# Which engine multiplies the queries by the cosine: GpSimd or VectorE

## The reference

```python
def apply_rope(x):                       # per head of 32 channels
    x1, x2 = (x[..., ::2], x[..., 1::2])
    out = jnp.stack([x1 * cos - x2 * sin, x1 * sin + x2 * cos], axis=-1)
    return out.reshape(x.shape)
q = heads(x @ Wq.T + bq)
k = heads(x @ Wk.T + bk)
v = heads(x @ Wv.T + bv)
g = jax.nn.sigmoid(heads(x @ Wg.T + bg))
q = jax.nn.elu(apply_rope(q)) + 1.0
k = jax.nn.elu(apply_rope(k)) + 1.0
...
S = S + jnp.einsum('bhtd,bhte->bhde', ki, vi)      # a running state, chunks of 64 tokens
num = jnp.einsum('bhtd,bhde->bhte', qi, S)
den = jnp.einsum('bhtd,bhd->bht', qi, Z)[..., None] + 1e-06
out = g * num / den                                # then out @ Wo.T + bo
```

## Time and profile before

| | |
|---|---|
| time, median of 3 runs | 1132.95 us (1131.48 to 1133.48) |
| the profiled execution, its own time | 1128.95 us |
| its span | 1127.1 us |
| busy: PE, PEld, DVE, ACT, POOL | 91%, 72%, 64%, 36%, 26% |
| POOL L443, 64 instructions of 128x256 | 893 ns mean |
| POOL L447, 16 instructions of 128x512 | 21.6 us in all, 1349 ns mean |
| DVE L762, 16 instructions of 128x512 | 12.4 us in all, 775 ns mean |
| DVE L767, 32 instructions of 128x512 | 40.1 us in all, 1254 ns mean |

### The profile page before, as it was taken

One profiled execution on the slowest core, in us unless ns is written; L12 is line 12 of the kernel. 1 busy time (PEld: TensorE's weight loads), 2 busy tenths in 40 slices (PEclk: granted clock), 3 DMA queues, 4 the chain that ended last, 5 costly groups with the idle time before them and its releaser, 6 DMA issues.

```text
span 1127.1 us, 13755 instructions
## 1 busy us (share of the span) xinstructions
PE 1030.8 (91%) x4920; PEld 809.6 (72%) x4920; DVE 717.8 (64%) x1150; ACT 402.7 (36%) x623; POOL 295.3 (26%) x245
## 2 busy tenths in 40 slices
PE   3799999989999827999999899999999999999997
PEld 2577777767777625777768687777777877888885
DVE  4565786785576646957657867764976774554542
ACT  3234333323342233344443253434253434322231
POOL 2247674543224400201222200142110132200021
PEclk9899999999999968999999999999999999999999
DMA  7116664130021025243463152446143327134421
GB/s 261 62 61 232 214 232 146 61 104 10 10 92 31 1 78 225 99 161 111 163 219 123 39 210 103 170 158 233 39 158 134 133 79 276 57 140 154 172 66 56
DMA packets 47862, 142.98 MB, mean 127 GB/s; under 512 B 3497, under 2 KB 14633, under 8 KB 42161
## 3 DMA queue, kind: packets, MB, share of 16 engines
q1 hardware_dynamic: 28720, 118.71, 28.8%
q10 hardware_dynamic: 19072, 23.35, 6.4%
HBM read 114.66 MB, written 27.39 MB: 126 GB/s over the span
## 4 chain that ended last, share of the span: by engine, by line
PE 44%; DVE 13%; issue 3%; ACT 2%; POOL 1%; DMA 1%; DVEq 0%; ACTq 0%
PE f_h L106 7%; PE f_h L107 7%; PE f_h L108 7%; PE f_h L2172 4%; PE f_y L106 3%; PE f_y L107 3%; PE f_y L108 3%; DVE f_q_mem L1933 2%; DVE f_work L1913 1%; PE f_y L2362 1%; DVE f_work L1905 1%; PE f_z_sum L106 1%; PE f_z_sum L108 1%; PE f_z_sum L107 1%; PE f_z_second L107 1%
## 5 line engine op out<-in xcount | busy, mean ns | idle before, releaser
L106 PE MATMUL f_h<-f_xT_hi,f_up 128*128 128x512 f32 x352 | 140.5, 399 | 1.6 <-issue 0.9
L107 PE MATMUL f_h<-f_xT_hi,f_up 128*128 128x512 f32 x352 | 138.4, 393 | 0.0
L108 PE MATMUL f_h<-f_xT_lo,f_up 128*128 128x512 f32 x352 | 137.7, 391 | 0.0
L106 PE MATMUL ring<-w_hi,xT_hi 128*128 128x512 f32 x256 | 110.4, 431 | 24.4 <-POOL xT_lo L429 21.8
L1505 POOL TENSOR_TENSOR f_down_lo<-f_down_raw,f_down_hi 128x512 fp32r<-128x512 f32 x44 | 61.1, 1390 | 227.5 <-ACT f_down_hi L1555 227.5
L1710 ACT ACTIVATE f_work<-f_h 128x512 f32<-128x512 f32 x88 | 52.4, 596 | 171.4 <-PE f_h L2172 114.8
L1905 DVE TENSOR_TENSOR f_work<-f_work,f_weightT 128x512 f32<-128x512 f32 x88 | 65.1, 739 | 73.7 <-ACT f_work L1710 69.9
L1516 POOL TENSOR_TENSOR weights<-weights,f_rows 128x512 f32<-128x512 f32 (+1 forms) x24 | 31.9, 1360 | 299.9 <-ACT f_rows L1637 183.6
L1913 DVE TENSOR_TENSOR f_work<-f_h,f_work 128x512 f32<-128x512 f32 x88 | 60.8, 691 | 70.8 <-PE f_h L108 65.3
L107 PE MATMUL ring<-w_hi,xT_lo 128*128 128x512 f32 x256 | 103.7, 405 | 0.0
L108 PE MATMUL ring<-w_lo,xT_hi 128*128 128x512 f32 x256 | 103.5, 404 | 0.0
(11 more groups left out here) (306 smaller groups left out, 2244.0 us busy)
## 6 DMA issues: line engine op xcount, KB each, us to landing
f_up<-up_scratch SPq DMA_DIRECT2D x44, 1408.0 KB, 6.2
f_down_raw<-in_down_stream ACTq DMA_DIRECT2D x44, 256.0 KB, 3.6
f_x<-x_scratch SPq DMA_DIRECT2D x7, 1024.0 KB, 8.8
scaled_w<-in_up_stream SPq DMA_DIRECT2D x6, 704.0 KB, 5.4
up_scratch<-q_mem SPq DMA_DIRECT2D x6, 704.0 KB, 3.6
up_scratch<-scaled_w SPq DMA_DIRECT2D x6, 704.0 KB, 3.1
x_tok<-in_x SPq DMA_DIRECT2D x4, 1024.0 KB, 5.6
out<-f_x SPq DMA_DIRECT2D x8, 512.0 KB, 3.1
```

Of the source, the lines that this page charges most:

```text
L106: pe.matmul(out, lhs_hi, rhs_hi, start=start, stop=False)
L107: pe.matmul(out, lhs_lo, rhs_hi, start=False, stop=False)
L108: return pe.matmul(out, lhs_hi, rhs_lo, start=False, stop=stop)
```

## The change

The product of the queries with the cosine goes from GpSimd's `rotate` to VectorE's `rotated_sum`, which now does the same for queries and keys: it waits for the copy out of PSUM, makes the product, and then waits for the products with the sine (before, the keys' product stood behind that wait).

```diff
@@ rotate (GpSimd)
                     pool.tensor_tensor(b4[:, :, :, two], q4[:, :, :, 1 - two],
                                        sin[:, :, two].unsqueeze(1).to_broadcast([P, H, DK // 2]),
                                        ALU.mult).then_inc(rot_b_ready, 1)
-                if i == 0:
-                    pool.tensor_tensor(rot_a[:, 0:D].rearrange("p (h i) -> p h i", i=DK),
-                                       qk[:, 0:D].rearrange("p (h i) -> p h i", i=DK),
-                                       ropes[:, 0, t, :].unsqueeze(1).to_broadcast([P, H, DK]), ALU.mult)\
-                        .then_inc(rot_a_ready, 1)
@@ rotated_sum (VectorE)
                 half = bass.ts(i, D)
                 n = 2 * g + i + 1
+                k, _, done = own(g, (PQ, PK)[i])
+                dve.wait_ge(drained[k], PRIMED + done)
+                dve.tensor_tensor(rot_a[:, half].rearrange("p (h i) -> p h i", i=DK),
+                                  qk[:, half].rearrange("p (h i) -> p h i", i=DK),
+                                  ropes[:, 0, in_batch(g), :].unsqueeze(1).to_broadcast([P, H, DK]), ALU.mult)\
+                    .then_inc(rot_a_ready, 1)
+                dve.wait_ge(rot_a_ready, PRIMED + n)
                 dve.wait_ge(rot_b_ready, PRIMED + 2 * n)
-                if i:
-                    k, _, done = own(g, PK)
-                    dve.wait_ge(drained[k], PRIMED + done)
-                    dve.tensor_tensor(rot_a[:, half].rearrange("p (h i) -> p h i", i=DK),
-                                      qk[:, half].rearrange("p (h i) -> p h i", i=DK),
-                                      ropes[:, 0, in_batch(g), :].unsqueeze(1).to_broadcast([P, H, DK]), ALU.mult)\
-                        .then_inc(rot_a_ready, 1)
-                dve.wait_ge(rot_a_ready, PRIMED + n)
                 dve.tensor_tensor(rot_a[:, half], rot_a[:, half], rot_b[:, half], ALU.add).then_inc(rotated, 1)
```

## The result

The changed kernel takes 1139.07 us (median of 10 runs, 1136.99 to 1143.04), the kernel before 1131.97 us (10 runs beside them, 1130.32 to 1133.48). The ratio is 1.0067, with a 95% interval of 1.0054 to 1.0081: slower by 0.7%, some 7.6 us. The profiled execution took 1138.36 us, its span is 1136.4 us.

What follows compares the result with a forecast made beforehand. TensorE was taken to set the pace, its edges without room leading to VectorE's chain. 4.0 + 0.6 + 1.1 + 1.5 - 0.35 = +6.9 us, on the median 1132.95, gave 1139.8 us; range 1135.5 to 1144.

Steps and rivals of the forecast that it cites:

- TensorE sets the pace; the edges without room lead to VectorE: First part: TensorE busiest; in tiles 1 to 5 both its zero-room edges lead back to VectorE's queries'-sum-to-keys'-min chain.
- Tiles 1 to 5, 5 x 0.8: Each of these tiles: keys' sum ends 0.8 us later and TensorE follows, +4.0 us in all.
- The replay of the turns: Tile 1's VectorE and GpSimd turns, with one product more: keys' sum ends at 83.85 instead of 83.01, 0.8 us later.
- the rival of 1.78 per tile: Each added product costs a whole turn: tiles 1 to 5 cost 8.9 instead of 4.0, time 1146 us; chance 0.13.
- Tiles 6 and 11, 0.3 each: VectorE's wait for `att_hi` takes up half the product; TensorE already waits for the features; +0.6 us together.
- Tile 13, 1.1: Keys' chain 1.1 us later, delaying `q_mem`, for which TensorE already waits 1.82 us: +1.1 us, wait 2.9 us.
- The clock in tile 13, 1.5: Behind the 2.9 us wait in tile 13 the tensor clock falls, +1.5 us; unless it falls, 0.
- No other falls: Outside tile 13 the forecast added nothing for clock falls.
- The other tiles, 0: Tiles 0, 7 to 10, 12, 14: waits or TensorE's own lateness cover the product, 0; without that cover 0.7 us each.
- the price named for the cover gone: In the other tiles, 0.7 us each if what hides the product there were gone.
- The start, -0.35: Before the first features: one GpSimd turn goes, VectorE's product comes, features 0.35 us earlier; bounds -0.4 and +0.7.

Runs made afterwards that it cites:

- e1: Kernel before with the queries' cosine product left out altogether, on either engine (output differs): 1131.25 us, ratio 0.9988.
- e2: Kernel before, GpSimd keeping its product, with VectorE making it again into an unused spare tile at the changed kernel's place: 1140.86 us, ratio 1.0071.
- e5: Changed kernel with extra matmuls into the next ring bank, ahead of the query transposes of tiles 7 and 12 and transposes in tile 13: 1139.1 us, ratio 1.0056.
- e13: Kernel before, unchanged, run again for a third profile: 1133.92 us.
- e7: Changed kernel with the queries' product, sum and min ahead of `attend` instead of behind it, tile 8 excepted: 1131.1 us, ratio 0.9992.
- e10: Changed kernel with the queries' product, sum and min and the keys' product ahead of `attend`, tile 8 excepted: 1128.38 us, ratio 0.9959.
- e11: Kernel before with the queries' sum and min and the keys' product ahead of `attend`, tile 8 excepted, queries' product on GpSimd: 1124.38 us, ratio 0.9937.

## Why the prediction was right, and where it was off

The direction held, and so did the mechanism of the delays: VectorE's chain has no room and pays the product's own length. The size (6.9 us forecast, 7.1 by the medians, 7.6 by the ratio) came out near partly by luck, as the sum below shows. By its steps:

- *TensorE sets the pace; the edges without room lead to VectorE.* Right, shown by e1 and e2: GpSimd's list doesn't matter in the tiles.
- *Tiles 1 to 5, 5 x 0.8.* 5 x 0.7 = 3.5. The replay of the turns was right in kind, each duration within 0.3 us (1.78, 1.67, 1.12, 0.68, 1.17, 0.69). The product costs its own length, not another turn; the rival of 1.78 per tile is out. TensorE's new wait for `att_lo` was 0.39 us, not 0.6.
- *Tiles 6 and 11, 0.3 each.* 0.28 and 0.25. The reason was half wrong: TensorE waits there for the gate's PSUM bank (e5), which hangs on the same exponential as the features.
- *Tile 13, 1.1.* 1.1, and the wait of 2.9 us came as 2.94.
- *The clock in tile 13, 1.5.* 1.55, in four of four profiles.
- *No other falls.* This step failed. I had compared single waits with single rows, 1.82 us without a fall and 2.14 with one, and took the first as safe. A third profile of before has a fall behind 1.82 us and one behind 1.5, and none behind 2.1. With the extra 0.25 us in tiles 6 and 11 a fall came there in 7 of 8 profiles (7 of 10 with e5), about 0.5 and 0.75 more of one than before. The forecast had put nothing for it; the runs showed falls of 1.55 and 1.4 us there. The Trainium skill has in "TensorE: Matmul & The Clock Gate", Part 1, that the activity window is free-running, so that the point at which the clock changes (there, its rise at a kernel's start) varies from run to run. The three profiles of the kernel before agree for its falls: in tiles 8 and 15 twice and in 6, 13 and 15 once.
- *The other tiles, 0.* Wrong for tile 8. The forecast said that TensorE is itself late there; it was only so because the clock had fallen. In e13, without the fall, the stretch from the attention transposes of tile 8 to those of tile 9 takes 22.4 us; in the changed kernel, also without it, 23.1: 0.7 us, the price named for the cover gone. In the first pair of profiles a lost fall (-0.8) hides it.
- *The start, -0.35.* The first features do come 0.36 us earlier (14.07 us behind the first contested `w_lo` for 14.43), but TensorE's wait ahead of them is 5.23 us for 4.50, because its projections end earlier still, and the clock is low at once: the stretch at 1.2 GHz around it lasts about 10 us for 7. First qT comes only 0.1 us earlier. TensorE at 38.68 us shows it, 1.09 us for four transposes that took 0.63:

```profile
38.68 1.09 PE L1054 MATMUL ring<-ident,feat 128*128 128x128 f32 x4 [5.23 <-DVE feat L770]
```

Together: delays 3.5 + 0.3 + 0.25 + 0.7 + 1.1 = 5.85 us where 5.7 were forecast; the start -0.1 where -0.35 was; and the falls. From the first contested `w_lo` to the end of the first part the two profiles of the changed kernel take 8.9 us more than the three of the kernel before on the mean (400.1 for 391.2), so about 3.1 us are left for the falls, where 1.5 were forecast. The sum of delays was nearly exact, and the clock was the part under-sized: by its steps the forecast was about 2 us low. The time doesn't show this, because the second part, with the same instructions, took 711.6, 715.1 and 714.7 us in the three profiles of before and 711.9 twice in the two of the changed kernel, 1.9 us less on the mean. Nobody forecast that, and whether it is chance is open; in the time it hides what the step on the falls left out. The profiled execution of before, 1128.95 us, was near the fastest of all runs of that kernel.

## What to carry to other kernels

Look for the engine with no room, not for the one with the most work: a 0.68 us product moved off GpSimd cost 0.7 us in each tile where VectorE's chain ended just as TensorE needed it, though VectorE was idle a third of the time. Put work in the receiver's idle stretch before its wait, not behind it: the queries' part ahead of `attend` turned a loss of 0.7% into parity (e7), and with the keys' product there too into a gain of 0.4% (e10) and, with the queries' product back on GpSimd, 0.6% (e11). And where two engines take turns at a resource, replay the turns: here, with four instructions on GpSimd's side, an added instruction cost its own length, not a turn.

## What the runs showed of the hardware that I had not expected

- No length of a single wait tells these profiles with a fall of the clock from those without: 0 of 6 at 1.42 us, 3 of 6 at 1.55, 4 of 4 at 1.83 (but 1 of 6 at 1.82 elsewhere), 4 of 13 at the 2.1 us of tile 8. A fall cost 1.4 to 1.55 us in tiles 6, 11 and 13, and 0.8 in tile 8, where a later wait took up the rest. In tile 11 a delay of 0.25 us brought 0.75 of a fall, in all about 1.3 us, more than the 0.7 us delay of tiles 1 to 5; this rests on 10 profiles.
- Between executions, with identical instructions, the second part varies by almost 5 us (711.6 to 716.3 us over all profiles, 711.6 to 715.1 over the three of the kernel before), while the tiles of the first without a fall repeat to 0.1 us. For changes of under 0.5%, distances in the trace say more than the time does.
- Where VectorE and GpSimd take turns, both are slower: four `w_lo` took 5.25 us with five of GpSimd's products beside them and 4.16 with four, and GpSimd's cosine product took 1.74 us there for 1.30 at the median.
